# Reordering one attention chunk: next keys ahead of state products and scores, output projection one chunk later

## What is computed

```python
x = x + 0.5 * ffn(layernorm(x))              # gated: silu, two hidden layers with gelu, ternary weights
x = x + attn(layernorm(x))                   # linear attention, then gelu feed-forward (Wf1, Wf2)
x = x + 0.5 * ffn(layernorm(x))

# inside attn, 16 heads of 64, phi(v) = elu(v) + 1
Q, K, V = phi(h @ Wq), phi(h @ Wk), h @ Wv   # h = layernorm(x)
S, z = cumsum(K V^T over tokens), cumsum(K)
out = (Q S) / max(Q z, 1e-6)
x = x + out @ Wo
```

## Time and profile before

| what | value |
|---|---|
| three runs | 857.38, 858.56, 855.78 us |
| profiled execution, its time | 863.09 us |
| profiled execution, its span | 861.4 us |
| mean granted TensorE clock | 0.990 |
| PE busy | 798.1 us, 93% of the span |
| DVE busy | 558.9 us, 65% |
| ACT busy | 563.2 us, 65% |
| POOL busy | 364.7 us, 42% |
| attention stage | about 205 to 605 us, its last chunks woven with the feed-forward until about 632 us |

### The profile page before, as it was taken

The page is one execution under the profiler, slowest core; times in us unless marked ns, Lnnn a source line. Parts: engine busy times, 40 slices in busy tenths (PEclk is TensorE's granted clock), DMA queues, the critical chain, the costliest instruction groups (busy, mean ns, idle before and its releaser), DMA issues. The chain is left out here.

```text
span 861.4 us, 26994 instructions
## 1 busy us (share of the span) xinstructions
PE 798.1 (93%) x11458; PEld 676.0 (78%) x11458; DVE 558.9 (65%) x1290; ACT 563.2 (65%) x1024; POOL 364.7 (42%) x292
## 2 busy tenths in 40 slices
PE   1799999998899999999999999998989899999997
PEld 0688888877788888879889888887777678888886
DVE  7655564374866878677687876878777582818120
ACT  3687777757655555646556755555668477777774
POOL 4597979682100101010010100101266487979784
PEclk9999999999999999999999999999999899999999
DMA  7001120201001001010010101101023320201010
GB/s 256 0 25 56 44 64 10 79 8 49 16 3 39 16 4 52 3 40 16 3 52 3 42 14 39 53 4 40 27 81 95 96 60 13 62 12 50 1 50 26
DMA packets 56762, 34.55 MB, mean 40 GB/s; under 512 B 1984, under 2 KB 55232, under 8 KB 56640
## 3 DMA queue, kind: packets, MB, share of 16 engines
q1 hardware_dynamic: 56640, 32.79, 13.2%
HBM read 22.29 MB, written 10.49 MB: 38 GB/s over the span
## 5 line engine op out<-in xcount | busy, mean ns | idle before, releaser
L1157 ACT ACTIVATE ee<-ps 128x512 f32<-128x512 f32 x128 | 77.8, 608 | 89.2 <-PE ps L821 62.3
L1776 POOL TENSOR_TENSOR axs<-ay,axr 128x512 f32<-128x512 f32 x8 | 10.2, 1273 | 275.9 <-DVE ay L1572 275.9
L1659 POOL TENSOR_TENSOR alA<-full,ahA 128x512 fp32r<-128x512 f32 x74 | 100.0, 1366 | 42.6 <-DVE ahA L1324 35.7
L676 PE MATMUL ps<-ahA,wh 128*128 128x512 f32 x288 | 114.6, 398 | 1.4 <-POOL alA L1659 1.4
L1316 DVE SCALAR_TENSOR_TENSOR full<-ps,sc,gate 128x512 f32<-128x512 f32 x64 | 46.6, 747 | 106.5 <-PE ps L676 66.0
L676 PE MATMUL ps<-ahB,wh 128*128 128x512 f32 x288 | 113.3, 393 | 0.0
L676 PE MATMUL ps<-alA,wh 128*128 128x512 f32 x288 | 113.3, 393 | 0.0
L676 PE MATMUL ps<-alB,wh 128*128 128x512 f32 x288 | 112.2, 390 | 0.0
L1659 POOL TENSOR_TENSOR alB<-full,ahB 128x512 fp32r<-128x512 f32 x76 | 98.8, 1313 | 14.2 <-ACT ahB L1065 8.6
L1064 ACT ACTIVATE full<-ps,sc 128x512 f32<-128x512 f32 x86 | 59.5, 692 | 34.2 <-PE ps L676 24.4
L1158 ACT ACTIVATE rr<-ps 128x512 f32<-128x512 f32 x128 | 78.0, 609 | 0.0
(11 more groups left out here) (179 smaller groups left out, 2274.5 us busy)
## 6 DMA issues: line engine op xcount, KB each, us to landing
wst<-in_ternary SPq DMA_DIRECT2D x5, 512.0 KB, 8.2
stage<-in_attn SPq DMA_DIRECT2D x4, 512.0 KB, 4.9
xlnA<-x_scratch SPq DMA_DIRECT2D x8, 256.0 KB, 3.3
axr<-x_scratch SPq DMA_DIRECT2D x8, 256.0 KB, 3.3
yx_scratch<-ay SPq DMA_DIRECT2D x8, 256.0 KB, 2.3
xs_scratch<-axs SPq DMA_DIRECT2D x8, 256.0 KB, 2.4
xlnA<-yx_scratch SPq DMA_DIRECT2D x8, 256.0 KB, 3.2
xlnB<-yx_scratch SPq DMA_DIRECT2D x8, 256.0 KB, 3.4
```

The source lines that it names most:

```text
L676: ins = nc.tensor.matmul(b[:, :], w[:, col(k):col(k) + P], x_[:, k, :], start=(k == 0 and j == 0), stop=(k == ks[-1] and j == terms - 1))
L1157: nc.scalar.activation(ee[k][:, :], src[:, :], ACT.Exp).then_inc(*X["act"].step(f"e_{name}"))
L1659: return nc.gpsimd.tensor_tensor(dst, src, hi.bitcast(F32), ALU.subtract)
L1776: nc.gpsimd.tensor_tensor(axs[:, :, :], ay[:, :, :], axr[:, :, :], ALU.add).then_inc(*X["pool"].step(f"ys{i}"))
```

## The change

No instruction is added or taken away; they are put into another order on PE, ACT and DVE, and PSUM banks are handed out in that order. PE's chunk becomes: K of the next chunk, D and S of this one, WO of the half before (in c0 and c2), Q, V, I and O, Q, V, in c0 yT, KT, OT, and in c1 and c3 nT. ACT and DVE follow. In the last chunks the feed-forward's products stand in groups of four, and WO and yT of the last half come after them; in `ffn_dve` the last attention residual now stands ahead of `f_normalise(4)`.

The diff, cut to PE's and DVE's programs and to two lines of the plan (ACT's moves the same way):

```diff
@@ attention_plan @@
+                state_products(g)
+                scores((turn(), turn()), g)
...
+                if g and c % 2 == 0:
+                    job(turn(), f"WO{hh - 1}", "act", f"wf{hh - 1}")
...
@@ attention_pe @@
                 transposed_keys(0)
-                state_products(0)
-                scores(0)
                 for g in range(NC):
                     c, i, n, hh = g % Q, g // Q, g + 1, g // 2
                     more = n < NC
                     if more:
                         for h in range(2):
                             token_major("K", n, h)
-                    else:
-                        f_first(0, (0, 1))
-                    outputs(g)
+                    state_products(g)
+                    scores(g)
+                    if not more:
+                        f_first(0, range(KT))
+                    if g and c % 2 == 0:
+                        projected(hh - 1)
                     for j in range(2):
                         if hh + 1 < NHALF:
                             queries(hh + 1, 2 * (g % 2) + j)
                         if more:
                             token_major("V", n, j)
-                        if c == 0 and i and j == 0:
-                            back(i - 1)
+                        if j == 0:
+                            outputs(g)
+                    if c == 0 and i:
+                        back(i - 1)
                     if n + 1 == NC:
                         f_norm(0)
                     if more:
                         transposed_keys(n)
                     else:
-                        f_first(0, (2, 3))
-                        f_first(1, (0, 1))
+                        f_norm(2)
+                        f_first(1, range(KT))
                     transposed_outputs(g)
                     if n + 1 == NC:
                         f_norm(1)
-                    if more:
-                        state_products(n)
-                        scores(n)
-                    else:
-                        f_norm(2)
-                        f_first(1, (2, 3))
-                        f_last(0)
-                    if g % 2:
-
-                        after("dve", f"ol{g}.1")
-                        three(bank(f"WO{hh}")[:, 0:2 * P],
...
-                        if hh + 2 < NHALF:
-                            norm(hh + 2)
+                    if g % 2 and hh + 2 < NHALF:
+                        norm(hh + 2)
+                f_last(0)
+                projected(NHALF - 1)
@@ ffn_dve @@
                 for t in range(2, NT):
-                    f_normalise(t + 2)
                     if t == 2:
                         residual(NT - 1)
+                    f_normalise(t + 2)
@@ attention_dve @@
-                accumulated(0)
-                masked(0)
                 for g in range(NC):
...
                     if more:
-                        for h in range(2):
-                            phi(f"K{n}.{h}")
+                        phi(f"K{n}.0")
+                    accumulated(g)
+                    masked(g)
+                    if more:
+                        phi(f"K{n}.1")
                     else:
-                        f_stats(2)
-                        f_split(0, ("lo1",))
-                    for j in range(2):
-                        divided(g, j)
-                    if c == 1 and i + 1 < NT:
-                        once(i + 1)
+                        f_normalise(2)
+                        f_split(0)
+                    if n + 1 == NC:
+                        f_normalise(0)
                     for j in range(2):
                         if hh + 1 < NHALF:
                             phi(f"Q{hh + 1}.{2 * (g % 2) + j}")
-                        if c == 0 and i and j == 0:
-                            residual(i - 1)
+                        if j == 0:
+                            for k in range(2):
+                                divided(g, k)
+                            if c == 1 and i + 1 < NT:
+                                once(i + 1)
+                    if c == 0 and i:
+                        residual(i - 1)
                     if c == 1 and i + 1 < NT:
                         twice(i + 1)
...
                     for j in range(2):
                         low_outputs(g, j)
-                    if more:
-                        accumulated(n)
-                        masked(n)
                     if c == 0 and i + 1 < NT:
                         attention_stats(i + 1)
```

More of the change, by code:

```diff
@@ L920, in transposed_outputs, with projected @@
                     transposes(bank(f"OT{g}.{j}"), [ot[:, 2 * p:2 * p + 2, :] for p in range(4 * j, 4 * j + 4)], X["pe"], f"OT{g}.{j}")
+            def projected(hh):
+                after("dve", f"ol{2 * hh + 1}.1")
+                three(bank(f"WO{hh}")[:, 0:2 * P],
+                      [(wah[:, 3 * DA + p * P:3 * DA + (p + 1) * P], wal[:, 3 * DA + p * P:3 * DA + (p + 1) * P],
+                        oh[:, p, :], ol[:, p, :]) for p in range(PR)], f"WO{hh}")
             def back(i):
@@ L1193, in attention_first, with projected @@
                     norm(hh)
+            def projected(hh):
+                h = hh % 2
+                after("pe", f"WO{hh}")
+                if h == 0 and hh:
+                    after("pe", f"yT{hh // 2 - 1}")
+                nc.scalar.copy(ayf[:, h * 2 * P:(h + 1) * 2 * P], ps[X["banks"].bank[f"WO{hh}"]][:, 0:2 * P])\
+                    .then_inc(*X["act"].step(f"wf{hh}"))
             def attention_act():
@@ L1208, in attention_act @@
                             exp_relu(f"K{n}.{h}")
+                    else:
+                        f_gelu(0, range(KT))
+                    if g and g % 2 == 0:
+                        projected(hh - 1)
                     for j in range(2):
@@ L1231, in attention_act @@
                         f_norm(1)
[L1232 to L1244, removed]
-                            norm(hh + 2)
+                    if g % 2 and hh + 2 < NHALF:
+                        norm(hh + 2)
+                f_evacuate(0)
+                projected(NHALF - 1)
             tern_act(ffn1, attention_first)
@@ L1654, in _ @@
                 own = slice(half * DH, (half + 1) * DH)
-                nc.gpsimd.tensor_copy(mask[own, :, :], later[own, own].unsqueeze(1).to_broadcast([DH, PR, DH]))                    .then_inc(*S.step(f"mask{half}"))
+                nc.gpsimd.tensor_copy(mask[own, :, :], later[own, own].unsqueeze(1).to_broadcast([DH, PR, DH]))\
+                    .then_inc(*S.step(f"mask{half}"))
                 pool.wait_ge(*S.done(f"mask{half}", 0))
```

79 lines of the change are left out of this document (34 added, 45 removed).

## The result

| | before | after |
|---|---|---|
| median of the timed runs, us | 856.74 (855.78 to 858.56, 4 runs) | 869.73 (867.14 to 870.81, 4 runs) |
| ratio to before | | 1.0145, 95% interval 1.0116 to 1.0174 |
| profiled execution: time, span, granted clock | 863.09, 861.4, 0.990 | 869.48, 867.8, 0.992 |
| busy in the profiled execution: PE, DVE | shown ahead | 800.3, 559.5 |

The forecast was 861.1 us with a range of 852 to 867. The sign was right, the size was not: +13.0 us between the medians where the sum had +3.7. Run again beside the kernel before in a later comparison, the changed kernel took 867.99 us against 859.49, ratio 1.0094 (1.0076 to 1.0112), +8.5 us. The two profiled executions differ by 6.4 us.

A forecast was written before the change was run, and what follows sets the result against it. PE was taken to set the pace in the attention stage. The terms, -6.0 - 0.5 + 12.6 + 3.5 + 2.1 - 5.0 - 3.0, gave +3.7 us on the 857.4 us median: 861.1 us, range 852 to 867.

The forecast's parts named there:

- nT directly behind OT: In c1 chunks PE reaches nT before `axn` is ready and waits 1.8 us in tiles 0 to 6: +12.6 us.
- Waits that coincide: Two or three of seven new c1 nT waits, plus small ones, are covered by a late PE: -5 us.
- Rival 3: Nothing coincides: all 18.2 us of added waits are paid, +8.7 us, 866.1 us; chance 0.13.
- The stalls inside the scores: PE's seven stalls in the attention scores, 10.4 us, stay as they are: 0, bounds -6 and +3 us.
- The last chunks: In 605 to 640 us the 1.8 us `xnA` wait goes, and half the 2.4 us residual wait: -3.0 us.
- The banks: Second keys in c3 wait 0.5 us, seven times: +3.5 us; second OT in c0 0.3, seven times: +2.1.
- WO a chunk later: In c1 chunks WO's five waits, put down to `ol` and one state sum, go: -6.0 us.
- Keys ahead of D: In the first chunk K fills the 0.5 us that D waited for the values: -0.5 us.

The follow-up runs named there:

- two shifted runs: 64 matmuls more (128 PE instructions), once, ahead of the first chunk: in the kernel before 860.44 us, ratio 1.0015; in the changed kernel 869.69 us, ratio 1.0114.

## Why the prediction was wrong in its size

Point by point, by the steps of the sum:

- **nT directly behind OT, +12.6.** Right in mechanism and nearly in size: seven waits, 1.80, 1.79, 1.79, 1.01, 1.50, 1.48 and 1.51 us from start to start, 10.9 in all. From the end of the statistics to the end of `axn` DVE took 9.3 us (327.93 to 337.22), forecast 9.38. PE reached nT 10.5 us after the chunk's first key matmul and `axn` was ready after 12.3, forecast 10.6 and 12.4. Moving nT away removed these 10.9 us and the 2.8 of the c3 banks, added 3.1 of a new wait, and gave 10.7 us back.
- **Waits that coincide, -5.** Failed: none did. I had read the three c1 chunks of before without a WO wait as chunks in which PE is late by chance. The new wait is reached right behind OT, whose own input comes from the same DVE chain, so a late PE and a late DVE move together; this reason is argued. Rival 3 was right in this.
- **The stalls inside the scores, 0.** Failed: -5 to -7. I had named K directly ahead of D as a reason for up to -6 and then chose 0 because "the new order has the same two dense runs per chunk". The dense runs are the same; what precedes them isn't. The two shifted runs show this for the order as a whole; that it is K's 1.59 us of sparse instructions which gives the refill its time is argued, not shown.
- **The last chunks, -3.0.** Failed in sign: +3.0. The `xnA` wait went, as said. The step counted two waits of PE and overlooked that the change puts OT of the last chunk behind a norm and twelve products of another tile on PE and ACT. DVE waits for it there, and in the loop behind PE's transposes wait for DVE's `xn` (6.1 us in four waits between 640 and 690 us). One edit of that position gave 3.4 us back. The phrase "paced by DVE" in an expectation says too much: in the chain of that loop PE, ACT and DVE take turns.
- **The banks, +3.5 and +2.1.** 0.41 us in seven c3 chunks, 2.8, and 0.37 in seven c0 chunks, 2.6.
- **WO a chunk later, -6.0.** Right inside this change: no wait of WO for `ol` is left between 205 and 605 us. As a statement on the move alone it is wrong, by 17 us in the run that made it alone. In the change, the keys go ahead of D and S and take banks that are free; that this is what lets WO leave is argued.
- **Keys ahead of D, -0.5.** The wait is gone. At the other end a new one came: S of chunk 30 waits 1.0 us for `ol`, which I had not foreseen. It stands behind OT of chunk 29 and so is part of the end's 3.0.
- **What the sum left out.** Gaps too short to be rows of waits, each under 0.2 us beyond the pace of its block and most where one block follows another, sum to 2.4 to 3.1 us more in the changed order. The sum had no term for them.

With the measured sizes the attention stage is -6.0 - 0.5 + 10.9 + 2.8 + 2.6 - 6.1 = +3.7, and 6.1 to 6.8 with the short gaps; the table has 6.2. With the end's 3.0 that is 9.1 to 9.8, against 9.2 in the traces and 8.5 between the medians of the second comparison. That the +3.7 equals the forecast's total is chance. The sum of the record misses by 5 for the coincidences, by 6 for the end, and by 6 the other way for the stalls; so one failure hid about half of the other two. What of the first comparison's 13.0 us lies beyond 9 isn't explained by any trace.

The profiled execution of before, 863.09 us, lay 5.7 above the median then known and 3.2 above the later one of 859.9. I carried the offset over and found nothing against it; after's profiled execution lies at its median.

By the Trainium skill ("Runtime: NRT & Kernel Launch", section Instruction fetch mechanics) the crossing of blocks of 256 instructions is mostly hidden. The stalls' numbers modulo 256 confirm the block. The shifted runs show that in the kernel before 12 us are not hidden, and that in the changed order half of that is.

## What to carry to other kernels

A block on the bottleneck engine is also the cover of everything behind it: before moving one, list whose result, whose bank and whose copy ripened under it, and price those, not only the wait that it had itself. A wait at a fixed place, fed by the chain that feeds its neighbours, comes in every iteration, so don't discount it for coincidence. And at a seam between two stages, look for the last item of the old stage that has been put behind items of the new one: everything that the other engines have queued behind it waits too.

## What was not expected of the hardware

PE stalls inside dense runs of 64x64 matmuls, for 1.3 to 2.1 us in the kernel before and 0.4 to 2.3 us in the changed one, at places fixed by the instruction's position in the program: 128 instructions more, once, at the start, moved seven stalls, and left their sum as it was (11.9 and 12.4 us). The second thing is DVE's. The same normalisation `xn` took 1.10 or 3.08 us in one trace of the changed kernel:

```profile
614.50 1.10 DVE L1286 TENSOR_SCALAR xnB<-xlnB,bagB,rsB 128x128 f32<-128x128 f32 x4
...
643.87 3.08 DVE L1286 TENSOR_SCALAR xnA<-xlnA,bagA,rsA 128x128 f32<-128x128 f32 x4 [0.49 <-POOL rsA L1725]
```

From 614.5 us POOL runs nothing; from 643.8 its two subtractions of full tiles follow each other (1.29 and 1.28 us). In the trace of before the same holds: 1.11 us at 642.85, where POOL rests until 644.93, and 3.08 us at 626.99, with POOL busy from 627.35 on. The Trainium skill ("SBUF — State Buffer", section Who interferes with whom) says that the two engines share a port pair, and that where a DVE instruction uses both of its pairs, whoever issues first holds the shared one for the whole instruction. The rows agree. No run here varied it alone. It matters at the end of this kernel, since there PE waits for `xn`.
